# First attention: heads worked in pairs, and the key-side sum of probabilities formed by another operand order

## The reference, cut to what matters

```python
def _cross_head_proj(inputs, qw1, qw2, kw1, kw2, qdd, kdd):
    h_q = jnp.einsum('bnts,btin->btsi', inputs, qw1)
    out = inputs + jnp.einsum('btsi,btin->bnts', h_q, qw2)
    h_k = jnp.einsum('bnts,bsin->btsi', inputs, kw1)
    out = out + jnp.einsum('btsi,bsin->bnts', h_k, kw2)
    out = out + inputs * jnp.transpose(qdd, (0, 2, 1))[:, :, :, None]
    out = out + inputs * jnp.transpose(kdd, (0, 2, 1))[:, :, None, :]
    return out
logits = jnp.einsum('bnth,bnsh->bnts', q, k)
logits = _cross_head_proj(logits, pre_qw1, pre_qw2, pre_kw1, pre_kw2, pre_qdd, pre_kdd)
logits = jnp.where(mask, logits, jnp.finfo(jnp.float32).min)
probs = jax.nn.softmax(logits, axis=-1)
probs = _cross_head_proj(probs, post_qw1, post_qw2, post_kw1, post_kw2, post_qdd, post_kdd)
o = jnp.einsum('bnts,bnsh->bnth', probs, v)
```

## Time and profile before

| what | us |
|---|---|
| median of 3 runs | 1273.13 (1269.97 to 1276.78) |
| profiled execution, its own time | 1277.13 |
| span of its trace | 1275.3 |
| mean granted TensorE clock | 0.930 |

### The profile page before, as it was taken

How to read it: one execution, slowest core, us unless ns; L and a number is a source line. 1 busy time by engine, 2 the same in 40 slices (tenths; PEclk the granted TensorE clock), 3 DMA queues, 4 the chain that set the end, 5 groups by cost and what they waited for, 6 DMA issues and landing times.

```text
span 1275.3 us, 19146 instructions
## 1 busy us (share of the span) xinstructions
PE 1065.2 (84%) x6320; PEld 743.2 (58%) x6320; DVE 824.2 (65%) x2070; ACT 598.5 (47%) x1449; POOL 215.3 (17%) x179
## 2 busy tenths in 40 slices
PE   0889987988799888996978888878898965899995
PEld 0666666666676666665446566643333353788884
DVE  4489847894789658975508889567667641454552
ACT  3167715773477426763133333225566730554442
POOL 1010100110010101010733333400000004122222
PEclk9889988999999998996979999979999965999998
DMA  9999100000000000002437888523555607476772
GB/s 270 245 231 241 41 1 0 1 0 1 1 0 1 1 1 1 1 0 93 145 117 236 272 281 272 177 84 141 190 214 181 232 34 253 157 242 203 224 239 34
DMA packets 74878, 161.17 MB, mean 126 GB/s; under 512 B 10642, under 2 KB 56990, under 8 KB 70432
## 3 DMA queue, kind: packets, MB, share of 16 engines
q1 hardware_dynamic: 65904, 145.52, 37.1%
q0 software_dynamic: 8880, 14.60, 4.5%
...
## 4 chain that ended last, share of the span: by engine, by line
PE 42%; DVE 23%; DMA 13%; issue 10%; ACT 8%; POOL 2%; SPq 1%; DVEq 0%; ACTq 0%; POOLq 0%
PE ps L1487 39%; DMA out<-arena 7%; DMA arena<-in_w0all 2%; DVE arena L1037 2%; DMA made<-arena 2%; DVE arena L1001 2%; DVE arena L1320 2%; ACT arena L608 2%; POOL out L519 1%; DVE arena L1009 1%; DVE den L905 1%; ACT arena L593 1%; ACT arena L586 1%; DVE arena L985 1%; DVE arena L1017 1%
## 5 line engine op out<-in xcount | busy, mean ns | idle before, releaser
L1487 PE MATMUL ps<-arena 128*128 128x256 f16 (+16 forms) x4712 | 848.3, 342 | 69.3 <-ACT arena L601 14.9
L1487 PEld LDWEIGHTS ps<-arena 128*128 128x128 f32 (+8 forms) x4712 | 563.4, 151 | 268.9 <-issue 116.7
L1471 DVE CAST arena<-arena 128x256 f16<-128x256 f32 x120 | 36.8, 306 | 109.5 <-ACT arena L788 108.0
L1037 DVE SCALAR_TENSOR_TENSOR arena<-arena 128x128 f32<-128x128 f32 x240 | 95.7, 460 | 1.4 <-ACT arena L593 1.4
L1320 DVE TENSOR_REDUCE arena<-ps 128x4 f16<-128x1024 f32 (+1 forms) x48 | 58.8, 1228 | 49.3 <-PE ps L1487 49.3
L788 ACT ACTIVATE arena<-ps,arena 128x256 f32<-128x256 f32 x120 | 55.7, 475 | 58.2 <-PE ps L1487 57.9
L608 ACT ACTIVATE arena<-ident,arena 128x128 f32<-128x128 f32 x256 | 80.8, 387 | 0.0
L1001 DVE SCALAR_TENSOR_TENSOR arena<-arena,ps 128x128 f32<-128x128 f32 (+1 forms) x128 | 46.7, 406 | 40.2 <-PE ps L1487 39.5
L519 POOL DMA_INDIRECT out<-arena x30 | 47.2, 1574 | 144.9 <-DMA out<-arena 76.0
L489 POOL DMA_INDIRECT made<-arena x47 | 52.7, 1121 | 112.3 <-DVE arena L1233 110.5
L460 POOL TENSOR_TENSOR den<-den,backd 128x512 f32<-128x512 f32 x9 | 11.4, 1269 | 355.6 <-DVE euv L893 355.6
...
...
## 6 DMA issues: line engine op xcount, KB each, us to landing
...
```

Of the source, the lines that this page charges most:

```text
L1037: ins = dve.scalar_tensor_tensor(dst, prob[:, n % 3, tiles[tt]], w, dst, ALU.mult, ALU.add)
L1487: return pe.matmul(o, l, r, start=start, stop=stop, skip_group_check=shared)
```

## The change

The heads are worked two at a time.
- TensorE: `scores(p)` does the q times k matmuls of heads 2p and 2p+1 alternately (they lie in different 32-row groups and in different PSUM banks), then both masks, then the 2x6 matmuls of the key side. `values(p)` does the 32-column matmuls of both heads alternately, then the key-side sum of both, with the diagonal matrix as the loaded operand and the transposed probabilities streamed: four matmuls of 256, 128, 256, 128 columns per head in place of three of 256. h_k so comes out transposed already, in banks 6 and 7. Iteration p is scores(p), turn(2p-2), turn(2p-1), values(p-1).
- ScalarE: an iteration begins with both `turn_out`, then both `exps`, both `second_rank`, and `normalise` with `diagonals_post` for each head.
- VectorE: both first ranks, the maximum of the first head, `mix` of an older head, the maximum of the second, `invert`, the other `mix`, `invert`, both `diagonals_pre`, and the pieces of `extra` of both old iterations.
- Tail: the two copies to mixk, six transposes and their wait are gone; mixkT is copied straight from banks 6 and 7. On TensorE the transposes of owT and the vk products now stand ahead of the transposes of h_q and the v0 products. VectorE has no wait of its own for the vk products any more.

The diff, cut to its core:

```diff
@@ -613,27 +613,30 @@
-                for k in range(N0 + 2):
-                    if k < N0:
-                        exps(k)
-                    if k + 2 < N0:
-                        second_rank(k + 2)
-                    if k in SLICE_EXP:
-                        exp_slice(b * 2 + 1 + SLICE_EXP.index(k))
-                    if 1 <= k <= N0:
-                        normalise(k - 1)
-                        diagonals_post(k - 1)
-                    if k >= 2:
-                        turn_out(k - 2)
+                for p in range(N0 // 2 + 1):
+                    pair = (2 * p, 2 * p + 1)
+                    if p:
+                        turn_out(2 * p - 2)
+                        turn_out(2 * p - 1)
+                    for n in pair:
+                        if n < N0:
+                            exps(n)
+                    for n in pair:
+                        if n + 2 < N0:
+                            second_rank(n + 2)
+                    for n in pair:
+                        if n < N0:
+                            normalise(n)
+                            diagonals_post(n)
+                    for n in pair:
+                        if n in SLICE_EXP:
+                            exp_slice(b * 2 + 1 + SLICE_EXP.index(n))
...
                 act.wait_ge(pv_done, b * N0 + N0)
-                act.activation(mixk[:, 0:256], ps[:, 6, 0:256], ACT.Copy).then_inc(tail_act, 1)
-                act.activation(mixk[:, 256:768], ps[:, 7], ACT.Copy).then_inc(tail_act, 1)
                 act.activation(owT.rearrange("p (a g) t -> p a (g t)", a=2), ps[:, 4:6], ACT.Copy).then_inc(tail_act, 1)
                 for i in range(2):
-                    act.wait_ge(tail_pe, b * TAIL0 + 3 + i)
-                    act.activation(mixkT[:, i], ps[:, 2 + i, 0:384], ACT.Copy).then_inc(tail_act, 1)
+                    act.activation(mixkT[:, i], ps[:, 6 + i, 0:384], ACT.Copy).then_inc(tail_act, 1)
...
-                for k in range(N0 + 2):
-                    if k == 0:
-                        logits(k, lambda: diagonals_pre(2))
-                    elif k < N0:
-                        logits(k, lambda: invert(k - 1))
-                    elif k == N0:
-                        invert(k - 1)
-                    if 0 < k and k + 2 < N0:
-                        diagonals_pre(k + 2)
-                    if k >= 2:
-                        mix(k - 2)
-                    for step in extra.get(k, []):
+                for p in range(N0 // 2 + 1):
+                    if p < N0 // 2:
+                        first_rank(2 * p)
+                        dve.wait_ge(s_read, b * N0 + 2 * p + 1)
+                        first_rank(2 * p + 1)
+                        maximum(2 * p)
+                        dve.wait_ge(s_read, b * N0 + 2 * p + 2)
+                    if p:
+                        mix(2 * p - 2)
+                    else:
+                        diagonals_pre(2)
+                    if p < N0 // 2:
+                        maximum(2 * p + 1)
+                        invert(2 * p)
+                    if p:
+                        mix(2 * p - 1)
+                    else:
+                        diagonals_pre(3)
+                    if p < N0 // 2:
+                        invert(2 * p + 1)
+                    for n in (2 * p + 2, 2 * p + 3):
+                        if p and n < N0:
+                            diagonals_pre(n)
+                    for step in extra.get(2 * p, []) + extra.get(2 * p + 1, []):
                         step()
...
-                def scores(n):
-
-                    pe.wait_ge(dg_pre, b * N0 + n + 1)
-                    if n >= 2:
-                        pe.wait_ge(s_read, b * N0 + n - 1)
-                    rows, g = slice(32 * (n % 4), 32 * (n % 4) + 32), n // 4
-                    o = ps[:, n % 2]
-                    mm(o[:, 0:P], qsT[rows, g, 0:P], ksT[rows, g, 0:P], True, False, True)
-                    mm(o[:, P:384], qsT[rows, g, P:], ksT[rows, g], False, False, True)
-                    mm(o[:, 0:384].rearrange("p (a j) -> p a j", a=3)[:, 0::2], identb[:], spread(causal[:], 1, 2),
-                       False, False, True)
-                    for blk, (tt, s) in enumerate(CAUSAL):
-                        for i in range(2):
-                            ins = mm(o[:, blk * P:(blk + 1) * P], rankkT[:, i, blk * P:(blk + 1) * P],
-                                     diag_pre[:, n % 4, 2 * s + i], False, blk == 2 and i == 1, True)
-                    ins.then_inc(s_ready, 1)
+                def scores(p):
+
+                    pair = (2 * p, 2 * p + 1)
+                    if p:
+                        pe.wait_ge(s_read, b * N0 + 2 * p)
+                    for tt, cols in enumerate((slice(0, P), slice(P, 384))):
+                        for n in pair:
+                            rows, g = slice(32 * (n % 4), 32 * (n % 4) + 32), n // 4
+                            mm(ps[:, n % 2, cols], qsT[rows, g, tt * P:(tt + 1) * P], ksT[rows, g, 0:(tt + 1) * P],
+                               tt == 0, False, True)
+                    for n in pair:
+                        mm(ps[:, n % 2, 0:384].rearrange("p (a j) -> p a j", a=3)[:, 0::2], identb[:],
+                           spread(causal[:], 1, 2), False, False, True)
+                    for n in pair:
+                        pe.wait_ge(dg_pre, b * N0 + n + 1)
+                        for blk, (tt, s) in enumerate(CAUSAL):
+                            for i in range(2):
+                                ins = mm(ps[:, n % 2, blk * P:(blk + 1) * P], rankkT[:, i, blk * P:(blk + 1) * P],
+                                         diag_pre[:, n % 4, 2 * s + i], False, blk == 2 and i == 1, True)
+                        ins.then_inc(s_ready, 1)
...
-                def values(n):
-
-                    pe.wait_ge(t_read, b * N0 + n + 1)
-                    pe.wait_ge(dg_post, b * N0 + n + 1)
-                    if n == 0:
+                def values(p):
+
+                    pair = (2 * p, 2 * p + 1)
+                    pe.wait_ge(t_read, b * N0 + 2 * p + 2)
+                    if p == 0:
                         pe.wait_ge(values_ready, b + 1)
-                    pT = probT[:, n % 2]
                     vals = vs.rearrange("p t n e h -> p t n (e h)")
-                    o = ps[32 * (n % 4):32 * (n % 4) + 32, 4 + n // 8, (n // 4 % 2) * T:(n // 4 % 2 + 1) * T]
-                    mm(o, vals[:, 0, n], pT[:, 0:2 * P], True, False, True)
-                    mm(o[:, P:], vals[:, 1, n], pT[:, 2 * P:], False, True, True)
-                    d0 = diag_post[:, n % 4, 0:2].rearrange("p i j -> p (i j)")
-                    d1 = diag_post[:, n % 4, 2:4].rearrange("p i j -> p (i j)")
-                    last = n == N0 - 1
-                    mm(ps[:, 6, 0:256], pT[:, 0:P], d0, n == 0, last, True)
-                    mm(ps[:, 7, 0:256], pT[:, P:2 * P], d0, n == 0, last, True)
-                    mm(ps[:, 7, 256:512], pT[:, 2 * P:], d1, False, last, True).then_inc(pv_done, 1)
-
-                for k in range(N0 + 3):
-                    if k < N0:
-                        scores(k)
-                    if 2 <= k <= N0 + 1:
-                        turn(k - 2)
-                    if k >= 3:
-                        values(k - 3)
-
-
+                    for s in range(TT):
+                        for n in pair:
+                            at = n // 4 % 2 * T
+                            o = ps[32 * (n % 4):32 * (n % 4) + 32, 4 + n // 8, at + s * P:at + T]
+                            mm(o, vals[:, s, n], probT[:, n % 2, 2 * s * P:(2 + s) * P], s == 0, s == 1, True)
+                    for n in pair:
+                        pe.wait_ge(dg_post, b * N0 + n + 1)
+                        pT = probT[:, n % 2]
+                        last = n == N0 - 1
+                        for i in range(2):
+                            mm(ps[:, 6 + i, 0:256], diag_post[:, n % 4, i], pT[:, 0:2 * P], n == 0, False, True)
+                            ins = mm(ps[:, 6 + i, 256:384], diag_post[:, n % 4, 2 + i], pT[:, 2 * P:], False, last, True)
+                        ins.then_inc(pv_done, 1)
+
+                for p in range(N0 // 2 + 1):
+                    if p < N0 // 2:
+                        scores(p)
+                    if p:
+                        turn(2 * p - 2)
+                        turn(2 * p - 1)
+                        values(p - 1)
+
...
+                pe.wait_ge(tail_act, b * 3 + 1)
+                for tt in range(TT):
+                    for g in range(4):
+                        pe.transpose(ps[:, 4 + tt, g * P:(g + 1) * P], owT[:, g, tt * P:(tt + 1) * P], ident[:])
+                pe.wait_ge(tail_act, b * 3 + 3)
+                for tt in range(TT):
+                    terms = [(i, s) for i in range(2) for s in range(tt + 1)]
+                    for j, (i, s) in enumerate(terms):
+                        blk = tt + s
```

(21 more changed lines are left out.)

29 lines of the change are left out of this document (14 added, 15 removed).

## The result

| | before | after |
|---|---|---|
| median of 20 runs each, one chip, us | 1274.12 (1265.47 to 1285.06) | 1286.33 (1281.37 to 1289.8) |
| ratio to before | 1 | 1.0098 (95% interval 1.0081 to 1.0114) |
| profiled execution's own time / span | 1277.13 / 1275.3 | 1284.52 / 1282.7 |
| mean granted clock | 0.930 | 0.910 |

What follows compares the result with a forecast made beforehand. It took PE as the head loop's bound before, VectorE close behind, and VectorE after. Head loop -5.2, tail +3.4 and clock +3.9 sum to +2.1 us per batch, +8.4 for four: 1281.5 us against 1273.13, range 1266 to 1292.

Steps and rivals of the forecast that it cites:

- PE's pace: Head loop on PE: 8.0 us of work per pair against 10.0, plus 0.75 us waiting for copies, 8.75 us.
- Overlap of the narrow matmuls: Values and scores on PE: two heads' narrow matmuls run two at a time, 0.65 us each in place of 1.3.
- VectorE's pace: Head loop: VectorE sets the pace, 9.65 us per pair against 10.6; six pairs give -5.7 us per batch.
- Start of the loop: Before the first values: both copies of the pair come earlier, -1.5 us per batch, bounds 0 and -3.
- two holes: PE's waits at the loop's end and in the tail: half clock after them adds 2.8 and 1.1 us per batch.
- End of the loop: From the start of values(6) to the loop's end: 13.9 us in place of 11.7, taken as +2 us per batch.
- Tail: From the last key-side matmul to VectorE's first sum: 9.2 us in place of 5.8, +3.4 us per batch.
- half clock costs little: Rival on both holes: half clock costs 1.4 and 0.5 us, +0.1 us per batch, 1273.5 us; chance 0.27.
- Faster, pairs at PE's pace: Rival in the head loop: VectorE isn't the bound, pairs pass at 8.75 us, -3.3 us per batch, 1260 us; chance 0.15.
- No overlap: Rival on PE: narrow matmuls overlap partly or not at all, up to 1.3 us more per pair, 1296 us; chance 0.08.

Runs made afterwards that it cites:

- e5_slices_after: Kernel after with all pieces of the next batch's recurrence moved behind the head loop; 1373.57 us (one run).
- e8_apart: Kernel after with each head's wide matmuls put between the narrow matmuls of the pair's two heads; ratio to before 1.0348.
- e9_warm_drain: Kernel after with unread matmuls only at the end of the head loop, none in the tail; ratio to before 1.0049.
- e2_warm: Kernel after with unread matmuls added in both holes, at the end of the head loop and in the tail; ratio to before 0.9982.
- e1_tail: Kernel after with the old order in the tail, h_q's transposes first and vk products last; ratio to before 0.997.
- e3_serial: Kernel after with a pair's narrow matmuls issued one head after the other, though they still ran side by side; ratio to before 1.0078.
- e7_tail_warm: Kernel after with the old tail order and unread matmuls in both holes; ratio to before 0.9897.
- e10_spread: e7_tail_warm with the recurrence's pieces dealt out evenly over the pairs, first deal; ratio to before 1.0012.

## Why the prediction was right, and what was mis-sized

Right: the direction, and the reason for it. The pairs gain, and the tail's order with the half clock takes more than that back. Per batch, forecast against measured (+2.1 against 140.0 - 136.5 = +3.5; by the medians' ratio 12.5/4 = +3.1):

- **PE's pace.** 8.0 us of work and 0.75 of wait: e5_slices_after passes pairs at 8.8, with 32.7/4 = 8.2 us of work and 2.6/4 = 0.65 of wait. Right.
- **Overlap of the narrow matmuls**, scores included: shown by the groups, 0.6 us against 1.2 in e8_apart. The prediction weighed a rule of the Trainium skill ("TensorE: Matmul & The Clock Gate", on packing), that a weight load overlaps running matmuls only where the row group differs, and read it as two heads' values in series. That would have been 1.2; the group took 0.6.
- **VectorE's pace.** Forecast 9.65 us per pair, measured (61.0 - 2.5)/6 = 9.75 without the half clock over the first values: six pairs are worth 58.5 - 63.6 = -5.1 us, not -5.7. It is an average of 8.8 and 9.0 us on one side and 10.6 and 12.5 on the other, since the pieces come in lumps. VectorE in order of time, the worst one:

```profile
392.07 1.27 DVE L1022 TENSOR_TENSOR arena<-ident,arena 128x512 f32<-128x512 f32 x2
393.25 1.76 DVE L908 RECIPROCAL den<-den 128x128 f32<-128x128 f32 x2
...
396.97 1.26 DVE L862 TENSOR_TENSOR_SCAN num<-dec,ekv 128x256 f32 x2
398.15 0.71 DVE L1005 SCALAR_TENSOR_TENSOR arena<-arena,ps 128x128 f32<-128x128 f32 x2
```

  4.9 us of pieces pass between the diagonals of one pair and the next first rank, the next diagonals come late, and PE waits for them at 404.35, 1.8 us.
- **Start of the loop.** Forecast -1.5. The first values come 3.2 us earlier, but 2.5 us of that returns as the half clock, which before was over when they began and now lies on them: -0.7. The paragraph on the clock priced two holes and had this stretch at nothing; it is the largest gap of the sum, 0.8 us. That a pair pays for it in full is seen in e9_warm_drain's third batch, where the first values take 6.14 us in place of 7.00 and the first pair 10.44 in place of 11.29; for the whole 2.5 us it is an estimate from that.
- **The clock inside the loop.** The prediction wrote of half clock only at the loop's end and in the tail. A further stretch came behind the longest wait for diagonals, and it cost no time. The third batch of e9_warm_drain passes the same place at full clock:

```profile
397.07 4.51 PE L1503 MATMUL ps<-arena 128*32 128x256 f32 x32 [0.64 <-ACT arena L601]
...
403.74 2.94 PE L1503 MATMUL ps<-arena 128*128 128x128 f32 x24 [1.83 <-DVE arena L1022]
...
409.08 4.51 PE L1503 MATMUL ps<-arena 128*32 128x256 f32 x32 [1.74 <-ACT arena L601]
...
418.51 3.66 PE L1503 MATMUL ps<-arena 128*32 128x256 f32 x24 [1.23 <-ACT arena L601]
```

  The 24 passes take 2.94 us in place of 4.54, but PE then waits 1.74 us for ScalarE's copies, and over the two pairs it is 418.51 - 397.07 = 21.44 us, as much as in the kernel after with the half clock (419.13 - 397.69 = 21.44). The fourth batch of e2_warm shows the same, 21.4 us. What lowers the clock there is open. The stretch comes in every batch of after, e1_tail, e3_serial and e7_tail_warm, and in three of four of e2_warm and of e9_warm_drain; but e10_spread waits 1.96 us for diagonals in another pair and keeps its full clock behind it, so such a wait is not enough.
- **End of the loop.** Forecast 13.9 us from the start of values(6) to the end, and 2.8 for the clock. Measured 435.7 - 419.1 = 16.6, of which 6.37 - 3.66 = 2.7 is clock: 13.9. Both right, though PE worked more in that hole than forecast and idled less (2.79 + 0.96 + 1.02 = 4.8 us, not 6).
- **Tail.** Forecast 9.2 us from the last key-side matmul to VectorE's first sum; measured 444.87 - 435.73 = 9.1. With the clock +4.5 forecast, +4.2 measured. e1_tail shows that the order is to blame: 4.8 us there.
- **The two holes.** Filling them gave 1.16 points, 14.8 us, 3.7 per batch (3.1 by the traces). By the prediction's prices it should have been 5.6: the growth of 3.9, and the 1.7 that the tail's hole cost before. In the third batch, from the start of the last values to the end of the batch, e2_warm takes 21.8 us against 26.6 in after, so 4.8 us are gone. But its first values come 1.4 us later in the batch (43.5 against 42.1), since half clock now lies over the 32 passes ahead of the loop. First after, then e2_warm:

```profile
338.11 5.50 PE L1503 MATMUL ps<-arena 128*128 128x128 f32 x32 [1.73 <-DVE arena L988]
```

```profile
332.30 6.88 PE L1503 MATMUL ps<-arena 128*128 128x128 f32 x32 [1.73 <-DVE arena L988]
```

  In e9_warm_drain's third batch the same passes take 8.47 us, 16 passes at the batch's start 4.78 in place of 3.62, and the first values come 4.1 us later. Why the clock falls there, no run tells.
- **Sum of the third batch.** Start -0.7, pairs -5.1, end of the loop +2.2 (13.9 against 11.7), its clock +2.7, tail with its clock +4.2: +3.3, against the forecast -1.5 - 5.7 + 2 + 2.8 + 4.5 = +2.1. No term is off by more than 0.8 us.

The profiled execution's own 1284.52 us against a sum of 1285.5 is closer than the terms deserve: its attention is 4.4 us above the forecast, and the part behind it is 5.4 us shorter for no reason that lies in the change. That is luck.

The rivals: "half clock costs little" is refuted by e2_warm. "Faster, pairs at PE's pace" holds only without the pieces (e5_slices_after); with them the pace came out 0.1 us worse than forecast. "No overlap" happens only when it is forced, in e8_apart.
